# Edge stages of a graph kernel cut to tiles of 128 edges: filter work by tile, sums by pair in two PSUM banks

## The reference

```python
# layer 0, graph convolution, on layernorm(x)
C = 0.25 * (cos(edge_weight * pi) + 1.0)
W = (ssp(edge_attr_64 @ fw1.T + fb1) @ fw2.T + fb2) * C[:, None]
msg = (x @ w1.T)[src] * W
agg = segment_sum(msg, dst, n)
# layer 1, graph attention, on layernorm(x)
score = einsum('ehd,ehd->eh', q[dst], k[src]) * SCALE
ex = exp(score - segment_max(score, dst, n)[dst])
msg = (ex / segment_sum(ex, dst, n)[dst])[:, :, None] * v[src]
h_new = segment_sum(msg, dst, n)
```

## Time and profile before

| | |
|---|---|
| median of three runs | 2128.72 us |
| the profiled execution, its span | 2134.3 us |
| TensorE busy | 1761.5 us, 83% of the span |
| VectorE busy | 1539.6 us, 72% |
| ScalarE busy | 1070.3 us, 50% |
| GpSimd busy | 1160.5 us, 54% |
| gathers of the filter stage (L319) | 440, 453.4 us |
| gathers of attention (L1740) | 440, 476.1 us |
| HBM | 225.34 MB read, 42.50 MB written |

### The profile page before, as it was taken

One profiled execution on the slowest core, in us unless ns is written; L12 is line 12 of the kernel. 1 busy time (PEld: TensorE's weight loads), 2 busy tenths in 40 slices (PEclk: granted clock), 3 DMA queues, 4 the chain that ended last, 5 costly groups with the idle time before them and its releaser, 6 DMA issues. The chain is left out here.

```text
span 2134.3 us, 41549 instructions
## 1 busy us (share of the span) xinstructions
PE 1761.5 (83%) x10388; PEld 1537.1 (72%) x10389; DVE 1539.6 (72%) x2788; ACT 1070.3 (50%) x2353; POOL 1160.5 (54%) x1169
## 2 busy tenths in 40 slices
PE   3699999999999989828973868888888888866278
PEld 3499999999999979728972756666666766645267
DVE  5388888888888845643545849899999898847622
ACT  1677777777777726403420145445455454316133
POOL 0376666666666601462443457777777777512112
PEclk7799999999999989758996989999999999867579
DMA  3443333333333312133323566666666666524310
GB/s 96 133 121 111 104 108 108 104 107 108 105 106 108 98 31 80 69 124 98 119 75 98 193 185 189 189 188 188 193 191 186 190 187 188 148 65 141 115 38 29
DMA packets 132538, 267.55 MB, mean 125 GB/s; under 512 B 24030, under 2 KB 75888, under 8 KB 132407
## 3 DMA queue, kind: packets, MB, share of 16 engines
q0 software_dynamic: 63456, 191.61, 30.7%
q1 hardware_dynamic: 68534, 73.21, 11.2%
q10 hardware_dynamic: 416, 1.18, 0.2%
HBM read 225.34 MB, written 42.50 MB: 125 GB/s over the span
## 5 line engine op out<-in xcount | busy, mean ns | idle before, releaser
L319 POOL DMA_INDIRECT e_rows<-h_table,e_idx x440 | 453.4, 1030 | 214.1 <-issue 106.3
L1740 POOL DMA_INDIRECT a_rows<-kv_table,a_idx x440 | 476.1, 1082 | 135.8 <-issue 128.9
L619 PE MATMUL e_w<-w2h,e_hidl 128*128 128x256 f32 x880 | 247.7, 304 | 2.9 <-DVE e_msg L704 2.9
L589 PE MATMUL e_agg<-e_msg,e_hot 128*128 128x256 f32 x880 | 246.1, 402 | 0.0
L1822 PE MATMUL a_q<-q,a_spread 128*128 x880 | 233.7, 407 | 6.5 <-ACT a_spread L1782 6.3
L620 PE MATMUL e_w<-w2l,e_hidh 128*128 128x256 f32 x880 | 226.4, 280 | 0.0
L1853 PE MATMUL a_agg<-a_rows,x 128*128 128x264 f32 x880 | 226.2, 402 | 0.0
L704 DVE TENSOR_TENSOR e_msg<-e_w,e_rows 128x1024 f32<-128x1024 f32 x110 | 134.7, 1224 | 93.4 <-PE e_w L623 93.4
L1775 ACT ACTIVATE a_apart<-iota_n,dst_rel 128x128 f32<-128x128 f32 x440 | 140.6, 391 | 112.9 <-PE a_agg L1853 112.8
L1822 PEld LDWEIGHTS a_q<-q,a_spread 128*128 128x128 f32 x880 | 166.2, 199 | 38.9 <-issue 12.8
L1853 PEld LDWEIGHTS a_agg<-a_rows,x 128*128 128x128 f32 x880 | 168.2, 200 | 24.7
(11 more groups left out here) (456 smaller groups left out, 4221.4 us busy)
## 6 DMA issues: line engine op xcount, KB each, us to landing
e_ea<-in_eaT SPq DMA_DIRECT2D x220, 64.0 KB
m_rows<-expert_rows SPq DMA_DIRECT2D x32, 272.0 KB, 2.7
e_rows<-h_table,e_idx POOLq DMA_INDIRECT x440
a_rows<-kv_table,a_idx POOLq DMA_INDIRECT x440, 3.7
q_ab<-expert_out SPq DMA_DIRECT2D x50, 128.0 KB, 3.3
kv_table<-q_kv SPq DMA_DIRECT2D x25, 256.0 KB, 2.2
u_stage<-in_m_w SPq DMA_DIRECT2D x16, 256.0 KB
x<-in_x SPq DMA_DIRECT2D x1, 3200.0 KB, 13.9
```

What stands on the lines that cost most here:

```text
L319: c.nc.gpsimd.indirect_dma_start(out=rows[:, g.slot8, j, :], out_offset=None, in_=table, in_offset=bass.IndirectOffsetOnAxis(ap=idx[:, g.s ...
L589: last = mm(bank(wins[j]), hot[:, g.slot4, t, :], msg[:, g.slot4, t, :], start=False, stop=False, skip_group_check=True)
L619: mm(w, hidl[:, g.slot, cols[k]], w2h[:, k, :], start=(k == 0), stop=False)
L1740: nc.gpsimd.indirect_dma_start(out=rows[:, g.slot * IG + j, 0:2 * D], out_offset=None, in_=c.kv_dram, in_offset=bass.IndirectOffsetOnAxis( ...
```

## The change

- Tiles have 128 edges: NT = 392, NC = NT + NW - 1 = 416 columns (440 before), the same number for every table. `prepare` counts and picks over RC = 4 columns of tiles, makes the source indices of the filter tiles apart (`src_t`), and three packed words per group, with one field per tile: the windows (`g_row`), the ring slots of the rows (`s_row`), the targets of the copies (`k_row`).
- Filter work (edge values, gathers, z, w, product) goes by filter tile, in NTG = 98 groups; the sums go over the 416 columns in NIG = 104 groups. A tile that reaches into two windows is filtered once and added twice. Its product stands in place of the gathered rows, in a ring of 14 groups, and TensorE reads it by a slot that is known at run time only.
- Sums go by pair of tiles in both stages: an opening for the other bank of the window before (`last_window`) and one for the other bank of the pair's first window, two adding matmuls, and two ScalarE copies, one per tile; a copy that is superseded goes to a 26th, unused window.
- All loops are written out; window words are loaded where they are used (no `Ahead`).
- In attention the sums stay in the two banks of the window's parity: VectorE's adding is gone, and so is the clearing of `c.sums`; rescaling works on PSUM, by `grown = 1 + grow`; VectorE does the product of queries and keys ahead of that with the exponentials; ScalarE copies the sums. The adding matmuls of tiles 2 and 3 stand in the next step, between the queries. 26 chunks instead of 28.

The diff, cut to its core:

```diff
-CT = 2
-TE = CT * P
-NT = -(-(E + 1) // TE)
-EP = NT * TE
-NI = NT + NW - 1
-NC = NI * CT
-RT, RC = 98, 2
+RT, RC = 98, 4
+NT = RT * RC
+EP = NT * P
+NC = NT + NW - 1
 GA = 64
 IG = 4
-JG = IG // CT
+NTG = NT // IG
 NIG = NC // IG
+LATE = -(-(NW - 1) // IG)
...
+RING = 14
+RING_T = RING * IG
+W_BITS, S_BITS = 5, 6
...
+                for lo, hi, laps in lap_spans():
+                    last = v.tensor_scalar(turn[:, lo:hi], t_all[0:1, lo:hi], float(-laps * RING_T), None, ALU.add)
+                link(last)
+                link(v.tensor_scalar(slot[:, :], turn[:, :], RING_T - 0.5, float(-RING_T), ALU.is_gt, ALU.mult))
+                link(v.tensor_tensor(slot[:, :], slot[:, :], turn[:, :], ALU.add))
...
+                for n, (row, base) in enumerate(((w_all[0:1, :], W_BITS), (slot[:, :], S_BITS), (target[:, :], W_BITS))):
+                    link(v.tensor_copy(packed[:, n, :], row[:, 0:NC:IG]))
+                    for j in range(1, IG):
+                        link(v.scalar_tensor_tensor(packed[:, n, :], row[:, j:NC:IG], float(1 << (base * j)), packed[:, n, :], ALU.mult, ALU.add))
+                v.tensor_copy(c.g_row[:, :], packed[:, 0, :])
+                v.tensor_copy(c.s_row[:, :], packed[:, 1, :])
+                v.tensor_copy(c.k_row[:, :], packed[:, 2, :])
...
-                    last = nc.tensor.matmul(p_t[:, 0:NI], ones[:, :], after[:, k, :], start=(k == 0), stop=(k == RC - 1))
...
+                for k in range(RC):
+                    last = nc.tensor.matmul(p_c[:, 3, k * RT:(k + 1) * RT], rows_f[:, 0, k, :], c.ident[0:RT, 0:RT], start=True, stop=True)
+                last.then_inc(s_c, 1)
+                pe.wait_ge(s_pick, RC)
                 for a in range(3):
-                    for h in range(CT):
-                        for k in range(RC):
-                            last = nc.tensor.matmul(p_c[:, a, h:NC:CT], rows_f[:, a, k, h * P:(h + 1) * P], pick[:, k, :], start=(k == 0), stop=(k == RC - 1))
+                    for k in range(RC):
+                        last = nc.tensor.matmul(p_c[:, a, 0:NC], rows_f[:, a, k, :], pick[:, k, :], start=(k == 0), stop=(k == RC - 1))
...
+def unpacked(packed, bits, most):
+    return [((packed >> (bits * j)) & ((1 << bits) - 1)).with_bounds(min_val=0, max_val=most) for j in range(IG)]
+def windows_of(eng, c, n):
+    return unpacked(eng.value_load(c.g_row[0:1, n:n + 1], min_val=0, max_val=(1 << (W_BITS * IG)) - 1), W_BITS, NW - 1)
...
+                for g in (Group(n) for n in range(NTG)):
+                    need(sp, None, (s_el, g.n - 2), own=True)
+                    sp.dma_start(ea[:, g.slot3, :], A["eaT"][:, g.n * W2:(g.n + 1) * W2]).then_inc(s_ea[g.slot3], 16)
...
+                    need(pool, s_pg, (s_agg, PAIRS * (g.n - RING + LATE + 1) if g.n >= RING else 0))
+                    for j in range(IG):
+                        nc.gpsimd.indirect_dma_start(out=rows[:, g.ring * IG + j, :], out_offset=None, in_=c.h_dram,
+                                                     in_offset=bass.IndirectOffsetOnAxis(ap=c.src_t[:, g.n * IG + j:g.n * IG + j + 1], axis=0)).then_inc(s_rows[g.ring], 16)
...
-                def add_item(g, j, wins):
-                    need(pe, None, (s_msg, g.n + 1), (s_acc, g.n * JG + j), own=True)
-                    mm(other(wins[j])[:, 0:2], none[:, :], w2h[:, 0, 0:2], start=True, stop=False, skip_group_check=True)
-                    for half in range(CT):
-                        t = j * CT + half
-                        last = mm(bank(wins[j]), hot[:, g.slot4, t, :], msg[:, g.slot4, t, :], start=False, stop=False, skip_group_check=True)
+                for p in range(2):
+                    mm(ap[:, p, 0:D], none[:, 0:P], none[:, :], start=True, stop=False, skip_group_check=True)
+                last_window = [None]
+                def add_pair(a, half, wins, slots):
+                    need(pe, None, (s_msg, min(a.n + 1, NTG)), (s_hot, a.n + 1), (s_acc, a.n * PAIRS + half), own=True)
+                    first = 2 * half
+                    if last_window[0] is not None:
+                        mm(other(last_window[0])[:, 0:2], none[:, 0:P], none[:, 0:2], start=True, stop=False, skip_group_check=True)
+                    mm(other(wins[first])[:, 0:2], none[:, 0:P], none[:, 0:2], start=True, stop=False, skip_group_check=True)
+                    for j in range(first, first + 2):
+                        last = mm(bank(wins[j]), hot[:, a.slot4, j, :], flat(rows[:, bass.ds(slots[j], 1), :]), start=False, stop=False, skip_group_check=True)
                     last.then_inc(s_agg, 1)
...
+                    last_window[0] = wins[first + 1]
+                for r in range(-5, NIG + 1):
+                    a, g, z = Group(r - 1, NIG), Group(r + 1), Group(r + 5)
+                    if a.real():
+                        wins, slots = windows_of(pe, c, a.n), slots_of(pe, c, a.n)
+                        add_pair(a, 0, wins, slots)
...
-                    if real(a) and not real(g):
-                        add_item(a, 1, sums)
-                    if real(g):
+                    if g.real():
                         need(pe, None, (s_hl, g.n + 1), (s_msg, g.n), own=True)
                         for j in range(IG):
-                            if j == 1 and real(a):
-                                add_item(a, 1, sums)
+                            if j == 1 and a.real():
+                                add_pair(a, 1, wins, slots)
...
+                def keep(a, half, wins):
+                    need(act, s_ag, (s_agg, a.n * PAIRS + half + 1))
+                    for j in (2 * half, 2 * half + 1):
+                        last = nc.scalar.copy(flat(c.sums[:, bass.ds(wins[j], 1), 0:D]), bank(wins[j]))
+                    last.then_inc(s_acc, 1)
...
-                        v.tensor_tensor(msg[:, g.slot4, :, :], wp[:, :].rearrange("p (a d) -> p a d", a=IG), rows[:, g.slot8, :, :], ALU.mult).then_inc(s_msg, 1)
...
+                        own = rows[:, g.ring * IG:(g.ring + 1) * IG, :]
+                        v.tensor_tensor(own, wp[:, :].rearrange("p (a d) -> p a d", a=IG), own, ALU.mult).then_inc(s_msg, 1)
...
-                nc.gpsimd.memset(c.sums[:, :, :], 0.0).then_inc(s_clr, 1)
...
+                def keep(m, half, wins):
+                    need(act, s_ag, (s_agg, m.n * PAIRS + half + 1))
+                    for j in (2 * half, 2 * half + 1):
+                        last = nc.scalar.copy(flat(c.sums[:, bass.ds(wins[j], 1), :]), bank(wins[j]))
+                    last.then_inc(s_acc, 1)
+                wins = None
+                for i in steps:
+                    if real(Edges(i.n - LAG - 1)):
+                        keep(Edges(i.n - LAG - 1), 1, wins)
...
-                        nc.scalar.copy(idx[:, g.slot, :], c.src_i[:, bass.ds(g.n * IG, IG)]).then_inc(s_idx, 1)
...
+                        wins = targets_of(act, c, m.n)
+                        keep(m, 0, wins)
...
+                def add_pair(m, half, wins):
+                    rescaled = (s_rs, 2 * (m.chunk + 1)) if m.place == 0 and half == 0 else (s_rs, 0)
+                    need(pe, None, (s_msg, m.n + 1), (s_acc, PAIRS * m.n + half), rescaled, own=True)
+                    if last_window[0] is not None:
+                        mm(other(last_window[0])[:, 0:2], none[:, 0:P], none[:, 0:2], start=True, stop=False, skip_group_check=True)
+                    mm(other(wins[2 * half])[:, 0:2], none[:, 0:P], none[:, 0:2], start=True, stop=False, skip_group_check=True)
+                    for j in (2 * half, 2 * half + 1):
+                        t = m.slot * IG + j
+                        last = mm(bank(wins[j]), hot[:, t, :], rows[:, t, D:ROW], start=False, stop=False, skip_group_check=True)
+                    last.then_inc(s_agg, 1)
+                    last_window[0] = wins[2 * half + 1]
...
+                        queries((0, 1))
+                    if real(b):
+                        add_pair(b, 1, sums)
+                    if i.place == 2 and closed(ch):
+                        move_ex(ch)
+                    if real(g):
+                        queries((2, 3)).then_inc(s_q, 1)
...
-                        mm(ap[:, 1, 0:DM], none[:, 0:P], none[:, 0:DM], start=True, stop=False, skip_group_check=True)
-                        for j in range(JG):
-                            to = ap[:, 0, 0:DM] if j == 0 else ap[:, bass.ds(moved, 1), 0:DM].rearrange("p a d -> p (a d)")
-                            for half in range(CT):
-                                t = m.slot * IG + j * CT + half
-                                last = mm(to, hot[:, t, :], rows[:, t, D:ROW], start=(j == 0 and half == 0), stop=False, skip_group_check=True)
-                        last.then_inc(s_agg, 1)
+                        sums = windows_of(pe, c, m.n)
+                        add_pair(m, 0, sums)
...
-                        w = ahead.take(i.step, "sums", a.n)
```

(18 more changed lines are left out.)

415 lines of the change are left out of this document (171 added, 244 removed).

## The result

The changed kernel takes 2553.67 us (median of four runs, 2551.85 to 2557.34) against 2130.1 us of the kernel before beside it: a ratio of 1.199, 95% interval 1.197 to 1.201. It was forecast slower, by 67.6 us; it is slower by 424, far outside the range. The profiled execution spans 2555.6 us.

A forecast was written before the change was run, and what follows sets the result against it. TensorE was taken to bound the filter stage, no engine attention; the loop over ScalarE was to overtake TensorE. Prepare 7, filter -1.4, its drain +56, attention -11, its drain +17: +67.6, 2196.3 us, forecast's own range 2160 to 2225, overall 2110 to 2242.

The forecast's parts named there:

- some seven to eleven more register instructions per group on the loop: Filter stage, loop over ScalarE: unpacking bank and row slot of four tiles, 62 ns per instruction, taken as 0.45 us per group.
- the sequencer works ahead while the array is busy: Filter stage: the reason given for taking 0.45 us per group for register work and the second value load.
- 6.28 for the array: Filter stage: TensorE's own need per group, 6.16 us plus 0.12 for two more openings; below the loop's 6.9.
- The two double copies: Filter stage, loop over ScalarE: a second copy per pair costs 0.31 us, twice per group, 0.62.
- The loop was summed to 5.7 us: Attention, steady: openings, double copies, one-hot tiles and TensorE's turn; with 0.1 for rescaling 5.8 us per group, -11 us.
- the rescaling: Attention: each chunk's first pair waits for VectorE's rescaling in PSUM, 0 to 0.25 us per group, taken as 0.1.
- TensorE's sequencer becomes the bound: Rival: two value loads and their unpacking exposed, 7.3 us per filter group, 39 us more, 2235 us; chance 0.14.
- The signs: Expected in the trace: filter products 6.9 us apart, TensorE about 0.91 busy; wrong if TensorE full or drain pairs under 3 us.
- +56: Filter drain: 16 pairs of sums left alone, 3.4 us each at full clock, 4.4 behind it; 69.1 us against 13.2.
- Attention's +17: Attention drain: seven groups of two pairs at 4.4 us, 61.6 us against 44.2 before.
- Prepare: Preparation before the filter stage: wider tile counts and small instructions for packed words, +7 us, bounds 0 and 8.
- The rule of the Trainium skill: Filter loop: a 64-deep queue would hide the unpacking, leaving the loop at 6.46 us and the stage 43 us shorter.

The follow-up runs named there:

- fixed places: Changed kernel with bank, row slot and query window as constants on TensorE, so no value loads or register arithmetic for them in either edge stage: 2176.13 us.
- fixed places and no rescaling: Changed kernel with bank, slot and window as constants and the rescaling of the crossing window's sum in attention left out: 2128.44 us.
- the version with loads earlier: Changed kernel, register arithmetic done once without moves behind the last three w tiles' dispatch, the filter's two loads behind z's dispatch: 2248.88 us.
- the version with values ahead: Changed kernel with register arithmetic done once into registers ahead of the wait for ScalarE's copy, four address instructions per pair behind it: 2625.4 us.

## Why the prediction was wrong, point by point

**The step that failed** is the term "some seven to eleven more register instructions per group on the loop" and the 0.45 us made of it. The runs showed 26 more at these lines (36 against 10, 22 more in all), 0.10 us apart in place of the 62 ns that I multiplied with, which leaves out the time between them. And it was taken that "the sequencer works ahead while the array is busy": it waits for ScalarE's copies ahead of each pair, twice per group, and all address work comes behind that wait. I had the list of uses in the diff (two openings, two banks, two slots per pair, each with shift, mask, parity and address) and did not count it out. Filter: 8.12 in place of 6.9; without register work 6.36, where I had 6.28 for the array. So register work and loads cost 1.76 us per group, where the sum had 0.45. The two double copies, 0.62 in the sum, did not make a loop of their own: with register work gone TensorE was full with them in place.

**The same step was missing in attention.** The loop was summed to 5.7 us without a term for more register work; the turn of 0.77 us in it was the filter stage's of before. With fixed places and no rescaling it measured 5.84. That is near, but not the same loop: inside a chunk this run's openings come 5.31 us apart per group (1503.58 to 1508.89), and the rest is lost where chunks begin. Then 38 register instructions replaced 4, worth 8.09 - 6.28 = 1.81 us with the loads. And the rescaling, put at 0.1 between 0 and 0.25, cost 0.44: I had bounded its wait by VectorE's own time, and it measured 2.20 us, with the product ahead of the three steps in it. 8.09 in place of 5.8, from first to last message 222 us more, where I had 11 less without the last seven groups.

**The rival named the place, not the size.** "TensorE's sequencer becomes the bound" stood at 7.3 us and 2235 us, with a chance of 0.14; its point against ("the array is full today with five of them per pair") took a small dose for a proof.

**The signs.** TensorE was to be busy 0.91 of the filter stage, and it was (699.61 of 770.00), by luck: 0.91 stood for 6.28 of 6.9 us and measured 7.4 of 8.12. ScalarE's copies were to end its idle time; in the steady stretch they end none of note, and the adding matmuls' weight loads have theirs put to "issue". The pace of the products, 8.12, was the plain miss. Of the two signs that were to prove the forecast wrong, TensorE full and pairs under 3 us apart, neither came.

**Drains.** +56 forecast for the filter stage, +59 measured; the pairs were 4.5 us apart, forecast 4.4 (the terms as they stand, 3.66 and 0.82, give 4.48). That sums alone are left there and each pair waits for copies was right. That the number came out was in part luck: register work was in it with 16 x 0.45 = 7 us and measured 17, the clock with 15 us and measured 10. Attention's +17 was +25 (the last seven groups and what follows: 72.6 us instead of 48.0).

**Prepare.** x's statistics start at 25.2 instead of 16.1 us, 9 later (forecast 7, bounds 0 to 8, so outside them); 5 of them are left at the first product.

**The rule of the Trainium skill.** The Trainium skill's "TensorE: Matmul & The Clock Gate", spec table, gives a queue 64 deep with weight loads pulled ahead. That the version with loads earlier hides most of 26 register instructions and two loads agrees with a queue of some depth. By that rule the unpacking was to be hidden in the changed kernel too, and there it was not: behind the wait its instructions begin at 503.7, when the copies have ended, and the matmuls they lead to are not yet queued.

**What is left.** The version with loads earlier stands 121 us over the kernel before, 111 by the two spans. By its rows: filter 42 us shorter, its drain 47 longer, attention's messages 91 longer ((1983.3 - 1281.1)/103 = 6.82 against 5.61 us per group), their end 23 longer, the stages between 10 shorter, the start 4 later. Which part of 6.82 - 5.84 is register work and which is rescaling was not separated in that version.

## What to carry to other kernels

A run-time address costs its engine's sequencer time for every shift, mask and address step, here 0.10 us each on TensorE, and the code shows them only if each use is counted out. Here they cost least where the engine's queue held work (6.49 us per filter group with 26 of them, 6.36 with none) and most behind a semaphore wait (8.12 with 36); so make the values in registers before the wait, at a place where long work has just been dispatched. Unused register work does not survive a build, so an experiment that adds some must use its result. An extra matmul costs its weight load too, however few its columns.

## What was not expected of the hardware

- In the version with values ahead, 1.9 us with 0.17 us of TensorE work were followed by 1.7 us at full clock and then by 3.6 us at a granted clock of 0.53; the rest of the group ran at 1.00. Gaps of 0.2 to 0.5 us in the changed kernel's filter stage left the clock at 1.00.
- Filling the drain's waits with matmuls of zeroes raised the granted clock from 0.53 to 1.00 and took 10 us off 69, so matmuls whose result nobody needs keep it up as well. In attention's drain of the kernel before the same idea raised it from 0.71 to 0.79 only, and gained nothing.
- Loads of a value by TensorE's sequencer, 0.302 us each and two per group, cost nothing in the filter stage with fixed places (6.36 with and without), and 0.52 us per group where they stood badly among register work (7.01 against 6.49).
- A matmul of two columns starts 0.03 us behind the one before it, but its weight load takes 0.11 us of the pace.
